# Moving small normalisation and convolution steps between the vector, scalar and pool engines of a Mamba, gated-recurrence and attention kernel

## The reference, cut to what matters

```python
x = x + mamba_block(layernorm(x))          # L0_attn_a: Mamba mixer and a ReLU feed-forward net
x = x + gated_recurrence(layernorm(x))     # L0_ffn: state c = f*c + i*g
x = x + attention(layernorm(x))            # L0_attn_b
x = x + gated_recurrence(layernorm(x))     # L0_ffn again

# inside mamba_block
h  = layernorm(x, ln1_g, ln1_b)
xi, z = split(rmsnorm(h, rms_w) @ in_proj_w)
xc = silu(causal_conv(xi, 4 taps) + conv_b)
delta = softplus((xc @ x_proj_w)[:64] @ dt_proj_w + dt_proj_b)
h_t = exp(delta_t * A) * h_{t-1} + delta_t * xc_t * B_t        # 256 features x 16 states
y   = (sum_n h_t C_t + D * xc) * silu(z)
h = h + y @ out_proj_w;  x = x + h
x = x + relu(layernorm(x, ln2) @ ffn_w1 + b1) @ ffn_w2 + b2
```

## Time and profile before

| | |
|---|---|
| median of three runs | 1722.15 us |
| the profiled execution | 1722.45 us |
| its span | 1720.6 us |
| around the span | 1.85 us |
| busy: PE, DVE, ACT, POOL | 1392.9, 1165.9, 885.4, 696.3 us |
| first scan of the first part | 84.4 us |
| end of the first part's last piece on DVE | about 884 us |

### The profile page before, as it was taken

The page is one execution under the profiler, slowest core; times in us unless marked ns, Lnnn a source line. Parts: engine busy times, 40 slices in busy tenths (PEclk is TensorE's granted clock), DMA queues, the critical chain, the costliest instruction groups (busy, mean ns, idle before and its releaser), DMA issues. The chain is left out here.

```text
span 1720.6 us, 17276 instructions
## 1 busy us (share of the span) xinstructions
PE 1392.9 (81%) x5520; PEld 659.7 (38%) x5520; DVE 1165.9 (68%) x1819; ACT 885.4 (51%) x1512; POOL 696.3 (40%) x407
## 2 busy tenths in 40 slices
PE   2332677979798989899973889999999999999994
PEld 1100343545444454545531223434443434343432
DVE  1296978978887888883125787676767667666325
ACT  3545456657574847453210465556555554645533
POOL 3466777859595967671313221212112121200000
PEclk9666788989999999999985799999999999999997
DMA  4424124151515151601035332423332332320034
GB/s 150 156 72 161 61 91 155 54 179 39 207 40 196 37 195 35 190 25 37 13 90 130 75 84 67 99 63 92 69 82 69 88 74 63 75 62 2 27 115 153
DMA packets 93785, 158.03 MB, mean 92 GB/s; under 512 B 8592, under 2 KB 74704, under 8 KB 90576
## 3 DMA queue, kind: packets, MB, share of 16 engines
q1 hardware_dynamic: 93696, 156.94, 30.8%
HBM read 110.91 MB, written 46.01 MB: 91 GB/s over the span
## 5 line engine op out<-in xcount | busy, mean ns | idle before, releaser
L1232 DVE TENSOR_REDUCE mx<-psum 128x1 f32<-128x512 f32 x512 | 345.4, 687 | 210.3 <-PE psum L1717 208.1
L1483 ACT ACTIVATE pw<-psum 128x512 f32<-128x512 f32 x512 | 300.2, 597 | 317.1 <-PE psum L1732 316.1
L868 POOL TENSOR_TENSOR hb<-ddb,bcb 128x1024 f32<-128x1024 f32 x128 | 304.9, 2403 | 128.4 <-DMA ddb<-dd 82.5
L503 DVE TENSOR_TENSOR_SCAN psum<-psum,hb 128x512 f32<-128x512 f32 x224 | 261.6, 1213 | 81.0 <-POOL hb L868 73.4
L1717 PE MATMUL psum<-kp,qp 96*128 96x512 bf16 x512 | 204.8, 401 | 45.8 <-DVE mx L1232 24.9
L694 ACT ACTIVATE psum<-ddb,A_neg 128x512 f32<-128x512 f32 x256 | 165.5, 680 | 132.7 <-DVE hb L506 68.8
L1732 PE MATMUL psum<-qp,kp 99*128 99x512 bf16 x512 | 197.5, 387 | 7.3 <-ACT pw L1483 6.0
L1625 POOL TENSOR_TENSOR rstd<-rstd,neg_half 128x4 f32<-128x4 f32 x16 | 16.3, 1019 | 410.8 <-DVE rstd L1217 410.8
L1743 PE MATMUL psum<-pw,v_sb 128*32 128x512 f32 x1024 | 138.1, 611 | 3.6 <-DVE ot L1256 2.3
L506 DVE TENSOR_TENSOR hb<-psum,bcb 128x1024 f32<-128x1024 f32 x112 | 137.2, 1225 | 3.9
L928 PE MATMUL psum<-back,w 128*128 128x512 f32 x256 | 115.3, 605 | 8.3 <-ACT back L710 8.3
(11 more groups left out here) (184 smaller groups left out, 2165.4 us busy)
## 6 DMA issues: line engine op xcount, KB each, us to landing
ddb<-dd SPq DMA_DIRECT2D x64, 512.0 KB, 8.9
bcb<-bc SPq DMA_DIRECT2D x32, 512.0 KB, 7.8
parts<-parts_sb SPq DMA_DIRECT2D x96, 128.0 KB
dd<-dd_out SPq DMA_DIRECT2D x8, 1024.0 KB, 4.0
qp<-parts SPq DMA_DIRECT2D x32, 256.0 KB, 7.7
kp<-parts SPq DMA_DIRECT2D x16, 384.0 KB, 4.6
x_front<-x_dram SPq DMA_DIRECT2D x8, 512.0 KB, 3.9
xh<-x_front SPq DMA_DIRECT2D x8, 512.0 KB, 2.9
```

Of the source, the lines that this page charges most:

```text
L503: e.tensor_tensor_scan(to[:, g, :], a[:, g, :], h[:, g, :], 0.0, ALU.mult, ALU.add).then_inc(scan_ok, 1)
L868: e.tensor_tensor(hb[n % NHB], ddb[k % NSLOT][:, 1:2, :].to_broadcast([P, 2, L]), bcb[q][:, 0, :, :], ALU.mult).then_inc(bx_ok, 1)
L1232: used.up(e.tensor_reduce(mx[u % 2][:, n:n + 1], bank(used.n % 2), AXIS.X, ALU.max))
L1483: e.activation(pw[n % NPW], bank(5 + n % 2), ACT.Exp, scale=HD ** -0.5).then_inc(exp_ok, 1)
```

## The change

Arithmetic is the same. Steps change engine, or change place in an engine's list:

- The last convolution tap goes from ACT to DVE, at the head of `conv`, and reads `xi_pad`.
- The subtraction in `mid_du` goes from POOL (L856) to DVE, behind L493.
- The small additions of epsilon and the negated means go from POOL to DVE, behind the moments; so does the small step on the sums of squares (new `front_square` on DVE at u=12).
- `front_norm` joins `front_apply` at u=8 on ACT; `front_sum` joins `front_scale` at u=9 on POOL.
- On DVE `back_sum` goes from u=1 to u=2 and `back_moments` from u=2 to u=3; POOL's `norm_power` follows to u=3. With scans at both, the order at u=2 is now scan, `back_sum`, `conv`.
- On ACT `mid_th` goes from u=3 to u=2, ahead of `gate_xwo`, which goes to u=3; `back_apply` goes from u=3 to u=4, behind `gate_i`; `mid_soft` goes ahead of the last two `back_relu` at u=9.
- `gate_state` waits for both tanh of `gate_f` before its first step.

```diff
@@ dve_first
-                return ins
+                own.up(ins)
+                e.wait_ge(own.sem, own.n)
             def front_moments(b):
                 e.wait_ge(x_in[b % 2], 16 * (b // 2 + 1))
+                moments(x_front, f_stats, f_mv)
                 if b > 0:
                     e.wait_ge(xn_ok, b)
-                moments(x_front, f_stats, f_mv).then_inc(f_var, 1)
+                e.tensor_scalar(f_neg.unsqueeze(2), f_mv[:, :, 0:1], -1.0, None, ALU.mult)
+                e.tensor_scalar(f_rs[:, 0, :].unsqueeze(2), f_mv[:, :, 1:2], EPS, None, ALU.add)
+                e.tensor_scalar(f_rs[:, 1, :].unsqueeze(2), f_mv[:, :, 1:2], 1.0 + EPS, EPS * EPS, ALU.mult, ALU.add).then_inc(f_var, 1)
+            def front_square(b):
+                e.wait_ge(sq_ok, b + 1)
+                e.tensor_scalar(f_sq, f_sq, 1.0 / D, EPS, ALU.mult, ALU.add).then_inc(f_var, 1)
             def norm_moments(src, which, var):
-                moments(src, bg_stats[which], bg_mv[which]).then_inc(var, 1)
+                moments(src, bg_stats[which], bg_mv[which])
+                e.tensor_scalar(bg_neg[which].unsqueeze(2), bg_mv[which][:, :, 0:1], -1.0, None, ALU.mult)
+                e.tensor_scalar(bg_rs[which].unsqueeze(2), bg_mv[which][:, :, 1:2], EPS, None, ALU.add).then_inc(var, 1)
             def conv(b, f):
-                e.wait_ge(tap_ok, 2 * b + f + 1)
+                if b > 0 and f == 0:
+                    e.wait_ge(d_ok, b)
+                own.up(e.tensor_scalar(cv, xi_pad[:, f, TAPS - 1:], w(TAPS - 1), conv_half[:, 8 + f:9 + f], ALU.mult, ALU.add))
                 for k in range(TAPS - 1):
+                    e.wait_ge(own.sem, own.n)
                     ins = e.scalar_tensor_tensor(cv, xi_pad[:, f, k:k + L], w(k), cv, ALU.mult, ALU.add)
...
-                e.scalar_tensor_tensor(w_, w_, 1.0, feat(mid0), ALU.subtract, ALU.subtract).then_inc(part_ok, 1)
-                e.tensor_tensor(ln, ln, feat(mid1), ALU.add).then_inc(part_ok, 1)
+                own.up(e.scalar_tensor_tensor(w_, w_, 1.0, feat(mid0), ALU.subtract, ALU.subtract))
+                own.up(e.tensor_tensor(ln, ln, feat(mid1), ALU.add))
+                e.wait_ge(own.sem, own.n)
+                e.tensor_tensor(ln, ln, w_, ALU.subtract).then_inc(d_ok, 1)
...
-                ring_done(e, "gf", b, 1)
                 for f in range(NF):
-                    e.wait_ge(gth_ok, 4 * b + 3 + f)
+                    e.wait_ge(gth_ok, 4 * b + 4)
...
-                    if u == 1 and back:
+                    if u == 2 and back:
                         back_sum(i - 1)
-                    if u == 2 and back:
-                        back_moments(i - 1)
                     if u in (1, 2) and mid:
                         conv(i + 1, u - 1)
+                    if u == 3 and back:
+                        back_moments(i - 1)
...
+                    if u == 12 and front:
+                        front_square(i + 2)
@@ act_first
                 ins.then_inc(h_raw, 1)
-
-            def front_norm(b):
                 for t in range(NT):
...
-                    if b > 0 and f == 0:
-                        e.wait_ge(d_ok, b)
-                    e.activation(feat(mid0)[:, f, :], ring("xi", b, f), ACT.Identity, scale=conv_half[:, f * TAPS + TAPS - 1:f * TAPS + TAPS],
-                                 bias=conv_half[:, 8 + f:9 + f]).then_inc(tap_ok, 1)
                     e.activation(xi_pad[:, f, TAPS - 1:], ring("xi", b, f), ACT.Copy).then_inc(r_act, 1)
...
-                    if u == 2 and gate:
+                    if u == 2 and mid:
+                        mid_th(i + 1)
+                    if u == 3 and gate:
                         gate_xwo(i - 2)
-                    if u == 3 and mid:
-                        mid_th(i + 1)
-                    if u == 3 and back:
-                        back_apply(i - 1)
                     if u == 4 and gate:
                         gate_i(i - 2)
+                    if u == 4 and back:
+                        back_apply(i - 1)
...
+                    if u == 9 and mid:
+                        mid_soft(i + 1)
                     if u == 9 and back:
                         back_relu(i - 1, 6)
                         back_relu(i - 1, 7)
-                    if u == 9 and mid:
-                        mid_soft(i + 1)
-                    if u == 10 and front:
-                        front_norm(i + 2)
@@ pool_first
             def front_power(b):
-                e.wait_ge(f_var, b + 1)
-                own.up(e.tensor_scalar(f_rs[:, 0, :].unsqueeze(2), f_mv[:, :, 1:2], EPS, None, ALU.add))
-                own.up(e.tensor_scalar(f_rs[:, 1, :].unsqueeze(2), f_mv[:, :, 1:2], 1.0 + EPS, EPS * EPS, ALU.mult, ALU.add))
-                own.up(e.tensor_scalar(f_neg.unsqueeze(2), f_mv[:, :, 0:1], -1.0, None, ALU.mult))
-                e.wait_ge(own.sem, own.n)
+                e.wait_ge(f_var, 2 * b + 1)
...
             def front_rms(b):
-                e.wait_ge(sq_ok, b + 1)
-                own.up(e.tensor_scalar(f_sq, f_sq, 1.0 / D, EPS, ALU.mult, ALU.add))
-                e.wait_ge(own.sem, own.n)
+                e.wait_ge(f_var, 2 * b + 2)
...
             def norm_power(which, var, n, done):
                 e.wait_ge(var, n)
-                own.up(e.tensor_scalar(bg_rs[which].unsqueeze(2), bg_mv[which][:, :, 1:2], EPS, None, ALU.add))
-                own.up(e.tensor_scalar(bg_neg[which].unsqueeze(2), bg_mv[which][:, :, 0:1], -1.0, None, ALU.mult))
-                e.wait_ge(own.sem, own.n)
...
                 e.tensor_tensor(tok(T0), tok(T0), over_tiles(row("ln1_b")), ALU.add).then_inc(h_ok, 1)
-
-            def front_sum(b):
                 e.wait_ge(h_ok, b + 1)
                 e.wait_ge(xn_ok, b + 1)
                 e.tensor_tensor(x_front, x_front, tok(T0), ALU.add).then_inc(xh_ok, 1)
 
             def mid_du(b):
-                e.wait_ge(part_ok, 2 * b + 2)
-                e.tensor_tensor(dd_out[:, :, 0, :], dd_out[:, :, 0, :], dd_out[:, :, 1, :], ALU.subtract).then_inc(d_ok, 1)
                 e.wait_ge(d_ok, b + 1)
...
-                    if u == 2 and back:
-                        norm_power(0, b_var, i, b_rstd)
                     if u in (1, 2) and mid:
                         e.wait_ge(conv_ok, 2 * (i + 1) + u)
+                    if u == 3 and back:
+                        norm_power(0, b_var, i, b_rstd)
...
                         front_rms(i + 2)
-                        front_sum(i + 2)
```

More of the change, by code:

```diff
@@ L275, in build @@
             "f_var", "f_rstd", "h_raw", "h_ok", "xn_ok", "xh_ok", "sq_ok", "m_ok"))
-        tap_ok, conv_ok, tanh_ok, xc_ok, sz_ok, soft_ok, part_ok, d_ok, du_ok = (sem(n) for n in (
-            "tap_ok", "conv_ok", "tanh_ok", "xc_ok", "sz_ok", "soft_ok", "part_ok", "d_ok", "du_ok"))
+        conv_ok, tanh_ok, xc_ok, sz_ok, soft_ok, d_ok, du_ok = (sem(n) for n in (
+            "conv_ok", "tanh_ok", "xc_ok", "sz_ok", "soft_ok", "d_ok", "du_ok"))
         bx_ok, dA_ok, scan_ok, hc_dve, hc_pool = (sem(n) for n in ("bx_ok", "dA_ok", "scan_ok", "hc_dve", "hc_pool"))
```

## The result

The changed kernel takes 1742.16 us (median of four runs, 1739.43 to 1743.93) against 1722.3 (1721.01 to 1724.1, four runs beside it). The ratio is 1.0113, 95% interval 1.0096 to 1.0131: slower by 1.1%. The forecast was 1714, so the kernel is slower where a gain was expected, and outside the range. The profiled execution took 1739.67 with a span of 1737.8.

A forecast was written before the change was run, and what follows sets the result against it. Bound: a loop over DVE, ACT and PE with DMA latency each turn. Terms -2 - 5.5 - 5.6 - 2 + 2 + 1.7 + 2.7 + 0.6 = -8.1 took 1722.45 to 1714 us; range 1702 to 1727.

The forecast's parts named there:

- Up to `mid_xc`: From an iteration's opening scan to `mid_xc`: saved `back_sum` wait -2.5, taps +1.4, small steps +0.25, POOL lock +1.4; together +0.55.
- The paragraph on PE: PE within an iteration: idles 4.5 us in `gi`, `out` saves 2.9, `xp` at T+30.9 to T+32.8; 90.0 taken for iterations 2 to 5.
- +0.4 + 0.5 - 5.7: End of iteration 3: small steps +0.4, `gate_state` waiting for both tanh +0.5, vanished end stall with short PE wait -5.7.
- the additions: Extra time per iteration from the changed steps, set against the vanished stalls; 4.6 us taken in iterations 0 and 1.
- The end stall: DVE's wait for `ddb` before the next opening scan: falls to about 0.3 us, with `ddb` issued 8.1 after `du_ok`, not 15.3.
- the +1.4 that was taken: Just before `mid_xc`: DVE held up by a POOL product it shares SBUF with, between 0 and 2.33 us.
- The gap of 4.5 us in `gi`: PE idles inside `gi` because ACT empties `xwo` at T+22.2 instead of T+17.7, behind `mid_th`.
- +2.7: Iteration 8: `back_apply` and the tanh before it delay `bturn`, nothing covering them; up to 4.4 if PE is cold.
- PE did not stay fast: Rival: ACT empties `xwo` without PE slowing, iterations 2 to 5 take 88.4, total 1703; chance 0.14.
- the stall at the end did not stay: Rival: `xh` behind `dd_out` lands late, 4 us more in each of six iterations, total 1738; chance 0.04.
- PE waiting at both places: Rival: PE cold at the waits in `gi` and `gc`, 91.9 in iterations 2 to 5, total 1722, no telling gain; chance 0.14.
- POOL slipped into the convolution: Rival: if `ddb` 2 lands after about T+6, POOL's products delay `conv`, 7 iterations x 2.4 = 17 us, total 1731; chance 0.14.

The follow-up runs named there:

- Run 1: The changed kernel with `back_sum` back at u=1: 1725.48 us, ratio 1.0010 to the kernel before.
- run 2: The kernel before with only `back_sum` moved to u=2, `back_moments` and `norm_power` to u=3: 1741.22 us, ratio 1.0100.
- 7: The changed kernel with `back_sum` at u=1 and all small steps back on POOL: 1729.02 us, ratio 1.0025 to the kernel before.
- 17: The kernel before with the next loads ahead of the `xh` write, and only `mid_th` ahead of `gate_xwo` on ACT: 1692.12 us, ratio 0.9801.
- 6: The kernel before with only the early `front_norm` and `front_sum`: 1700.13 us, ratio 0.9852.
- 9: The changed kernel with `back_sum`, `back_moments`, `norm_power`, ACT's order and `mid_soft` at their old places: 1719.08 us, ratio 0.9966 to the kernel before.
- 4: The changed kernel with `back_sum` at u=1 and `gate_xwo`, `mid_th`, `back_apply` at their old places: 1725.89 us, ratio 1.0009 to the kernel before.
- 8: The changed kernel with `back_sum` at u=1 and `back_moments`, `norm_power` back at u=2: 1732.74 us, ratio 1.0048 to the kernel before.
- number 5: The kernel before with only SP's order changed, `bcb` and `ddb` loads issued ahead of the `xh` write: 1682.67 us, ratio 0.9757.
- 13: As number 5, with `back_apply` behind `gate_i` on ACT in iterations having mid and gate: 1684.25 us, ratio 0.9766 to the kernel before.
- 10: The changed kernel with all list places restored and the convolution taps back on ACT: 1709.54 us, ratio 0.9911 to the kernel before.
- 14: As number 5, with only the convolution taps moved to DVE: 1689.08 us, ratio 0.9797 to the kernel before.

## Why the prediction was wrong

**The step that failed** is in the part *Up to `mid_xc`*: "`back_sum` after scan 2 finds PE done: the wait of 2.05 and some 0.4 before it go, -2.5." It looked only at whom `back_sum` waits for, and not at who waits for `back_sum`. The wait did go, as forecast. But `back_sum` is the step that empties the first bank of `out`. The paragraph on PE used the same rule of three uses for `xwo` and `gi`, and had "with `out` at full speed it will at T+14.2" without checking `gturn`, which stands between. `xwo` ended at T+24.5 instead (362.66 + 6.52 - 344.67). Runs 1 and 2 show the price from both sides: 17 us, against a miss of 28. Run 1 moves `back_sum` alone; run 2 has `back_moments` and `norm_power` with it.

**The rest of the miss**, about 11 us, is in the sizes. Iteration 3, by stretches between scans, forecast beside number 1 (with that move undone) and the changed kernel, each as the difference to before:

| stretch | forecast | number 1 | changed |
|---|---|---|---|
| opening scan to scan 5 | +0.55 | +0.2 | +0.9 |
| scan 5 to scan 10 | +1.45 | +3.5 | +5.5 |
| scan 10 to scan 11 | +1.1 | +1.2 | +1.2 |
| scan 11 to the next opening scan | -4.8 | -4.0 | -4.0 |
| iteration | -1.7 | +0.9 | +3.6 |

(The forecast's last line is +0.4 + 0.5 - 5.7.) The second stretch was mis-sized. The forecast had `front_norm` in it, less 0.6. It left out the small steps L462 to L464, whose rows sum to 0.9 us in the changed kernel and 3.0 in number 1 there; without them (7) scan 10 comes at T+54.1 instead of T+55.4. And it took the ReLUs ahead of `front_apply` on ACT as punctual, though they wait for PE's products, which every pause of PE makes later: `front_apply` begins at T+49.0 before (401.73 - 352.75), T+50.7 in number 1 (395.09) and T+53.4 in the changed kernel (398.08). In the changed kernel the decay of unit 10 begins only at 402.01 and DVE waits 4.68. Two sums of the prediction do not come out of their parts, without much weight: the additions are 4.0 us in iteration 3 but 4.6 in iterations 0 and 1, and the parts named for scan 10 to scan 11 make 0.7, or 1.4 with the decay, where 1.1 was taken (1.2 measured).

**What held.** The end stall went to 0.26 or less from iteration 2 on, and `ddb` followed 7.3 us behind `dd_out` (forecast 8.1). The start, iterations 0, 1 and 6 came within 1.2 us each. `mid_xc` took 2.59, beside a product of POOL, which is the +1.4 that was taken; as that was a choice between 0 and 2.33, the exact hit is luck. The second tap of each iteration took 0.54 (forecast 0.7). The first took 0.97, 2.47, 2.31, 1.25, 0.83, 1.46 and 0.54 in iterations 0 to 6. So the tap can be held up by POOL, which the earlier trace rows had made look half unlikely, and the 14 taps took 13.6 us instead of 9.8. The gap of 4.5 us in `gi` was hidden in the changed kernel by the larger one ahead of `xwo`, but it appears as such in runs 1 and 17.

**From iteration 7 on** +9.5 stands against +5. Number 1 gives 5.2 us of it back, though PE's wait for `back_sum` in iteration 7 is only 1.21 us; how the rest comes about is not shown. In iteration 8 `back_apply` behind `gate_i` costs what was forecast: from `xwo` to `bturn` it is 13.3 us where it was 10.4, +2.9 against +2.7. In addition PE loses its clock, which the prediction had only as a bound: the products take 16.92 where they took 14.00.

```profile
821.06 1.09 PE L916 MATMUL psum<-ident,back 128*128 128x128 f32 x8 [2.74 <-ACT back L708]
823.25 16.92 PE L921 MATMUL psum<-back,w 128*128 128x512 f32 x32 [1.10 <-ACT back L720]
```

**The rivals.** None of the four decided. PE did not stay fast, and the stall at the end did not stay. With PE waiting at both places the prediction had 91.9 us per iteration; iterations 2 to 5 took 94.9. POOL slipped into the convolution in one iteration, number 2, where `ddb` 2 came at T+8.2, on the side of T+6 that the prediction gave for it:

```profile
256.59 4.84 POOL L862 TENSOR_TENSOR hb<-ddb,bcb 128x1024 f32<-128x1024 f32 x2 [5.86 <-DMA ddb<-dd]
```

```profile
256.92 2.31 DVE L481 TENSOR_SCALAR middle<-xi_pad,conv_half 128x512 f32<-128x512 f32 x1
259.27 4.29 DVE L484 SCALAR_TENSOR_TENSOR middle<-xi_pad,conv_half,middle 128x512 f32<-128x512 f32 x3
```

The tap waited for one product and the first of the three steps for the next; in the other iterations the three took 2.33. That is a few us in all, not the 17 of that rival. What did decide on the slow side, a ring bank emptied too late by DVE, was not among the rivals.

**Where the gain went.** Removing the stall with front_norm early is worth 24 us (6). Of the 42 that the rest takes back, the places in the lists are 23 (9 against the changed kernel), with `back_sum` the largest; the move of work to DVE, with the later `gate_state`, is 19, with the taps the largest. These do not add up piece by piece: undoing one place while another stays can move a wait elsewhere (4, 8), so the prices of single moves hold only in the kernel in which they were taken. Open is how the last 8 us of this part divide, of which `gate_state` is some 2.

**The better version** is the kernel before with the loads ahead of the `xh` write (1682.67), or that with `mid_soft` first (1680.32; the two can't be told apart): 2.4 to 2.5% faster than before, with no step moved to a busier engine. The earlier trace rows already held it. The stall was an order in SP's queue, and what the write of `xh` feeds comes later than `ddb`: it is read back two iterations on, and in number 5 DVE never waits for the next `x_front`.

## What to carry to other kernels

Before moving a step on one engine, ask what it waits for, which buffer it frees, and who is the next user of that buffer. In a ring with three banks, list the uses in order and write beside each the instruction that empties it. When a transfer is late because another stands ahead of it in the same queue, try the order of the queue first, before speeding up the work that makes the other one late.

## What the runs showed of the hardware

- A pause of 7.00 us on PE was followed by 8.40 us at a granted clock of 0.55; one of 4.53 by groups of 3.78 and 2.54 in place of 1.88. A wait of 1.81 inside `z` left the group behind it at 1.98 (13), while 2.59 there made 3.46 (5). The length of the wait alone does not tell: in number 1 the same 3.59 us was followed by 1.98, 2.58, 3.78 and 2.54.
- A DVE `tensor_scalar` on four elements per partition took 0.16 us, and 2.32 while POOL's product ran (number 1, L464). One tap over 512 elements took 0.54, or up to 2.47 where POOL's opening products were running; in iterations 0, 1 and 3 it ended 0.28 us behind POOL's product each time.
- Moving 16 taps from ACT, busy 873 of 1738 us in the changed kernel, to DVE, busy 1223, cost 9.5 and 6.4 us in two kernels (10 against 9, 14 against 5).
